# Layer 0's queries and keys written to DRAM ahead of the row maxima, layer 1's high and low parts a unit later, and the second router's norm derived from the first variance

## The reference, cut to what matters

```python
x = L0_attn_x
xn = _layernorm(x)
x = x + _L0_attn_ref(xn, ...) + _L0_ffn_ref(xn, ...)
xn = _layernorm(x)
x = x + _L1_attn_ref(xn, ...) + _L1_ffn_ref(xn, ...)
```

```python
mu = jnp.mean(x, axis=-1, keepdims=True)
var = jnp.var(x, axis=-1, keepdims=True)
xn = (x - mu) * jax.lax.rsqrt(var + LN_EPS) * ln_scale + ln_bias
logits = xn @ router_w.T + router_b
top_w, top_idx = jax.lax.top_k(logits, TOP_K)
```

## Time and profile before

| | |
|---|---|
| median of three runs | 497.09 us (496.85 to 499.26) |
| the profiled execution's own time | 498.41 us |
| its span in the profile | 496.7 us |
| granted TensorE clock, mean | 0.988 of full speed |
| busy: PE / weight loads / DVE / ACT / POOL | 88% / 62% / 65% / 48% / 37% |
| chain that ended last | PE 58%, DMA 12%, DVE 12%, issue 6%, SP's queue 4%, ACT 4% |

### The profile page before, as it was taken

How to read it: one execution, slowest core, us unless ns; L and a number is a source line. 1 busy time by engine, 2 the same in 40 slices (tenths; PEclk the granted TensorE clock), 3 DMA queues, 4 the chain that set the end, 5 groups by cost and what they waited for, 6 DMA issues and landing times.

```text
span 496.7 us, 9940 instructions
## 1 busy us (share of the span) xinstructions
PE 436.3 (88%) x3263; PEld 307.8 (62%) x3263; DVE 321.8 (65%) x988; ACT 240.1 (48%) x565; POOL 184.9 (37%) x234
## 2 busy tenths in 40 slices
PE   2568899997999899999999997999997999999985
PEld 1444446765666576665656655566557998998642
DVE  4554770117587777787877788767564666776665
ACT  2511355443655556553645435455463555555562
POOL 6570010002152543544445441666430444444100
PEclk9999999999999999999999999999997999999999
DMA  6447062323364653632236452142242122211233
GB/s 172 137 102 180 15 193 63 110 83 114 83 178 117 156 162 82 176 121 84 83 100 225 147 158 84 42 133 75 65 119 69 54 71 60 71 52 35 59 110 107
DMA packets 55216, 52.76 MB, mean 106 GB/s; under 512 B 5312, under 2 KB 50000, under 8 KB 55168
## 3 DMA queue, kind: packets, MB, share of 16 engines
q1 hardware_dynamic: 44208, 35.12, 25.4%
q10 hardware_dynamic: 8528, 12.03, 8.2%
q0 software_dynamic: 2432, 5.01, 3.4%
HBM read 33.09 MB, written 19.04 MB: 105 GB/s over the span
## 4 chain that ended last, share of the span: by engine, by line
PE 58%; DMA 12%; DVE 12%; issue 6%; SPq 4%; ACT 4%; POOL 3%; DVEq 0%; ACTq 0%; POOLq 0%
PE ps_P L1611 6%; PE ps_N L1743 5%; DMA scm<-MS 5%; DMA scr<-XQ 4%; PE ps_N L1544 4%; PE ps_M L1784 3%; PE ps_M L1753 3%; PE ps_P L1753 3%; PE ps_S L1743 3%; PE ps_M L1654 3%; PE ps_S L1589 3%; PE ps_N L1555 2%; PE ps_N L1550 2%; DVE NM L1140 2%; PE ps_S L1575 2%
## 5 line engine op out<-in xcount | busy, mean ns | idle before, releaser
L885 ACT ACTIVATE PT<-ps_S 128x512 f32<-128x512 f32 x192 | 112.3, 591 | 80.5 <-PE ps_S L1589 39.3
L1140 DVE TENSOR_REDUCE NM<-ps_N 128x2 f32<-128x512 f32 (+1 forms) x192 | 127.2, 680 | 35.5 <-PE ps_N L1550 22.7
L737 POOL TENSOR_SCALAR_AFFINE_SELECT PT<-PT 128x512 f32<-128x512 f32 x80 | 49.0, 636 | 139.2 <-ACT PT L885 139.2
L1544 PE MATMUL ps_N<-maskb,identb 128*128 128x256 bf16 (+1 forms) x192 | 62.0, 323 | 2.6 <-DVE NM L1140 1.7
L803 POOL DMA_INDIRECT yt<-LATE,EI x39 | 38.9, 997 | 56.3 <-DVE LATE L1378 46.6
L1611 PE MATMUL ps_P<-PT,VA 128*16 128x256 f32 (+1 forms) x1024 | 54.0, 328 | 0.4 <-ACT PT L885 0.4
L1550 PE MATMUL ps_N<-NS 96*128 96x512 f32 x96 | 52.8, 554 | 0.0
L1555 PE MATMUL ps_N<-NS 96*128 96x256 f32 (+1 forms) x128 | 49.4, 427 | 0.0
L1589 PE MATMUL ps_S<-NS 100*128 100x512 f32 (+1 forms) x96 | 46.2, 485 | 1.6 <-ACT PT L885 1.6
L1611 PEld LDWEIGHTS ps_P<-PT,VA 128*16 128x16 f32 x1024 | 23.3, 96 | 34.3 <-issue 20.5
L987 ACT ACTIVATE LATE<-ps_N,ucol 128x128 f32<-128x128 f32 x104 | 29.8, 369 | 27.4 <-PE ps_N L1743 26.0
(11 more groups left out here) (197 smaller groups left out, 845.1 us busy)
## 6 DMA issues: line engine op xcount, KB each, us to landing
scr<-XQ SPq DMA_DIRECT2D x24, 256.0 KB
NS<-scr SPq DMA_DIRECT2D x64, 96.0 KB
ROT<-in_L_ffn_W SPq DMA_DIRECT2D x16, 256.0 KB, 3.1
EW<-in_moe ACTq DMA_DIRECT2D x8, 512.0 KB, 3.8
scr<-XQ SPq DMA_DIRECT2D x24, 128.0 KB
NS<-scr SPq DMA_DIRECT2D x8, 384.0 KB
TS<-scr ACTq DMA_DIRECT2D x8, 384.0 KB
TS<-scr ACTq DMA_DIRECT2D x32, 96.0 KB
```

Of the source, the lines that this page charges most:

```text
L737: last = pool.affine_select(out=v, in_=v, compare_op=ALU.is_ge, fill=0.0, base=0, pattern=[[0, 4], [1, P]], channel_multiplier=-1)
L885: act.activation(PT[:, n % NPT, r, :], bank[s][:], ACT.Exp, scale=SCALE).then_inc(exp_ok, 1)
L1140: dve.tensor_reduce(to, x, AX.X, ALU.max, negate=True).then_inc(nm_ok, 1)
L1544: mm(diag, identb[:], maskb[:, None, :].broadcast_to((P, many, P)), start=True, stop=False, skip_group_check=True)
```

## The change

Three things change. First, the plan: in layer 0 `lo` comes behind unit 0's maximum and exponential and no longer ahead of them; in layer 1 `hi` moves from unit 0 to unit 1 (behind its exponential) and `lo` from the start of unit 1 to unit 2 (behind its maximum). Second, the item `stack` is split: `store` issues the four writes to scr, and `stack` waits for them and reads back. In layer 0 `store` stands ahead of `mrow` of half 1; in layer 1 it stands behind it, where the writes were. The reads of `again` move from units 3 to 7 to units 5 to 9. Third, the second norm: the variance of XN is now computed as v * rstd * rstd on two numbers per row, and its mean is taken as zero, so one fused instruction per tile makes the logits.

```diff
         for u in range(12):
             if u == 0:
                 add("qk", a)
-                add("hi", a)
-            if a and u == a[0]:
-                add("lo", a)
+                if t < NB:
+                    add("hi", a)
...
             add("max", b, u)
             add("exp", c, u // 3, u % 3)
+            if u == 0 and t < NB:
+                add("lo", a)
+            if u == 1 and t >= NB:
+                add("hi", a)
+            if u == 2 and t >= NB:
+                add("lo", a)
...
             if u == 1:
+                if t < NB:
+                    add("store", a)
                 add("mxt", c, 1)
                 add("mrow", c, 1)
+                if t >= NB:
+                    add("store", a)
                 add("stack", a)
                 add("ocp", d, 1)
...
-            if 3 <= u < 8 and b and b[0] == 0:
-                add("again", b, u - 3)
+            if 5 <= u < 10 and b and b[0] == 0:
+                add("again", b, u - 5)
...
-            def stack(L, b):
+            def store(L, b):
 
                 n = seq(L, b)
                 rows = P if L == 0 else NKV * HD
...
                 sp.dma_start(scr[L][b][1][0:rows, 2, :], xq[0:rows, 2, :]).then_inc(scr_w, 16)
+
+            def stack(L, b):
+
+                n = seq(L, b)
                 sp.wait_ge(scr_w, 64 * (n + 1))
...
-                pool.tensor_scalar(vpe[:, s], mv2[:, s, 1], EPS, 1.0, ALU.add, ALU.mult).then_inc(vpeb_ok, 1)
+                pool.tensor_scalar(vpe[:, s], var2[:, s], EPS, 1.0, ALU.add, ALU.mult).then_inc(vpeb_ok, 1)
...
-                dve.tensor_copy(rc[:, 0, :], bank["M0"][:, 0:E1])
-                dve.tensor_tensor(rc[:, 1, :], bank["M0"][:, E1:2 * E1], rbb[:], ALU.add).then_inc(rc_ok, 1)
+                dve.tensor_tensor(rc[:], bank["M0"][:, 0:E1], rbb[:], ALU.add).then_inc(rc_ok, 1)
...
-                dve.wait_ge(xnb_ok, 2 * b + 2)
-                for i in (2 * b, 2 * b + 1):
-                    last = dve.bn_stats(stats2[:, i, :], XN[:, i, :])
-                link(last)
-                for i in (2 * b, 2 * b + 1):
-                    last = dve.bn_aggr(mv2[:, i, :], stats2[:, i, :])
-                last.then_inc(mvc_ok, 1)
+
+                s = slice(2 * b, 2 * b + 2)
+                link(dve.tensor_tensor(var2[:, s], mv[:, s, 1], rstd[:, s], ALU.mult))
+                dve.tensor_tensor(var2[:, s], var2[:, s], rstd[:, s], ALU.mult).then_inc(mvc_ok, 1)
...
-                link(dve.tensor_tensor(dlt[:, s, :], bc(mv2[:, s, 0:1]), bc(rc[:, 0:1, :]), ALU.mult))
-                dve.tensor_tensor(ex[:, s, :], bank[f"M{b % 2}"][:, 0:2 * E1].rearrange("p (a e) -> p a e", e=E1), dlt[:, s, :],
-                                  ALU.subtract).then_inc(lg1_ok, 1)
+                for q in range(TPB):
+                    i = 2 * b + q
+                    last = dve.scalar_tensor_tensor(out=lg[:, i, :], in0=bank[f"M{b % 2}"][:, E1 * q:E1 * (q + 1)],
+                                                    scalar=rstd2[:, i:i + 1], in1=rc[:], op0=ALU.mult, op1=ALU.add)
+                last.then_inc(lg1_ok, 1)
                 dve.wait_ge(lg1_ok, b + 1)
-                link(dve.tensor_tensor(dlt[:, s, :], ex[:, s, :], bc(rstd2[:, s, None]), ALU.mult))
-                link(dve.tensor_tensor(lg[:, s, :], dlt[:, s, :], bc(rc[:, 1:2, :]), ALU.add))
...
-                mm(M0[:, 0:E1], ones, rwS[:], start=True, stop=True)
-                mm(M0[:, E1:2 * E1], ones, rwB[:], start=True, stop=True).then_inc(full["M0"], 1)
+                mm(M0[:, 0:E1], ones, rwB[:], start=True, stop=True).then_inc(full["M0"], 1)
```

More of the change, by code:

```diff
@@ L361, in build @@
         rbb = sb("rbb", [P, E1])
-        rc = sb("rc", [P, 2, E1])
+        rc = sb("rc", [P, E1])
         stats = sb("stats", [P, NT, 6])
@@ L368, in build @@
         mhalf = sb("mhalf", [P, NT])
-        stats2, mv2 = sb("stats2", [P, NT, 6]), sb("mv2", [P, NT, 2])
+        mv2, var2 = sb("mv2", [P, NT, 2]), sb("var2", [P, NT])
         rstd2 = sb("rstd2", [P, NT])
@@ L631, in attention @@
                 for item in plan:
+                    if item[0] == "store":
+                        store(*item[1:])
                     if item[0] == "stack":
@@ L1260, in normalise_x @@
                         .then_inc(xnb_ok, 1)
-                dve.wait_ge(xnb_ok, 2 * b + 2)
-                for i in (2 * b, 2 * b + 1):
-                    last = dve.bn_stats(stats2[:, i, :], XN[:, i, :])
-                link(last)
-                for i in (2 * b, 2 * b + 1):
-                    last = dve.bn_aggr(mv2[:, i, :], stats2[:, i, :])
-                last.then_inc(mvc_ok, 1)
+                s = slice(2 * b, 2 * b + 2)
+                link(dve.tensor_tensor(var2[:, s], mv[:, s, 1], rstd[:, s], ALU.mult))
+                dve.tensor_tensor(var2[:, s], var2[:, s], rstd[:, s], ALU.mult).then_inc(mvc_ok, 1)
             def logits(b):
-                s = slice(2 * b, 2 * b + 2)
-                def bc(x):
-                    return x.broadcast_to((P, TPB, E1))
                 await_full(dve, f"M{b % 2}", ("pl", 1, b))
                 dve.wait_ge(rstdc_ok, b + 1)
-                dve.wait_ge(mvc_ok, b + 1)
                 dve.wait_ge(rc_ok, 1)
-                link(dve.tensor_tensor(dlt[:, s, :], bc(mv2[:, s, 0:1]), bc(rc[:, 0:1, :]), ALU.mult))
-                dve.tensor_tensor(ex[:, s, :], bank[f"M{b % 2}"][:, 0:2 * E1].rearrange("p (a e) -> p a e", e=E1), dlt[:, s, :],
-                                  ALU.subtract).then_inc(lg1_ok, 1)
+                for q in range(TPB):
[3 more added lines that the diff above has]
+                last.then_inc(lg1_ok, 1)
                 dve.wait_ge(lg1_ok, b + 1)
-                link(dve.tensor_tensor(dlt[:, s, :], ex[:, s, :], bc(rstd2[:, s, None]), ALU.mult))
-                link(dve.tensor_tensor(lg[:, s, :], dlt[:, s, :], bc(rc[:, 1:2, :]), ALU.add))
                 for i in (2 * b, 2 * b + 1):
```

## The result

The changed kernel takes 494.65 us in the median of 17 runs (492.27 to 495.73), the kernel before 498.21 beside it; the ratio is 0.992, interval 0.9903 to 0.9937, so 0.6 to 1.0% faster. The time lies on the forecast of 494.6 us, but the forecast took 2.4 us off a median of 497.09, and measured side by side the kernel before takes 1.1 us more than that and the change takes off 3.6.

The account below looks back on a forecast made before the run. PE, busy 88% of the span, was taken as the bound, with DVE's chain to the division a second critical path. 1.27 + 0.4 + 0.5 + 0.35 + 0.2 - 0.35 = 2.4 us off 497.09 gave 494.6 us, range 490.5 to 498.0.

Parts of the forecast that it names:

- of the 0.8 us only 0.12 are kept: Stages 8 to 11: PE's unit-2 wait of 0.8 us becomes a wait of `ott` for the division, gaining 0.12 per stage.
- The term of 0.5 us: Layer 1, stages 8 to 11: 4 x 0.12 = 0.5 us gained in all.
- Stages 13 and 14: Layer 1, stages 13 to 15: the wait for an exponential is at most 0.6 us; no gain credited.
- Stage 12: `rank` waits for DVE's values (VA), which stand behind the low part: 0.35 us lost, halfway between 0.06 and 0.70.
- 1.3 us to spare, no cost: Layer 0, stage 5: half 1's maxima, behind four writes, are read back by 160.1; PE needs them at 161.4.
- The two waits of 1.27 us: Starts of stages 5 and 6: waits for the maxima of 0.41 and 0.86 us should go, 1.27 us gained.
- 1.67 us credited: Layer 0: 1.27 us from the maxima waits at stages 5 and 6, plus 0.4 from earlier scores in stages 4 and 7.
- Second norm and constants: DVE saves 4 to 7 us in stages 4 to 11, nothing on PE's path; smaller router constants gain 0.2 us.
- SP's chain at the experts: Start of layer-1 experts: PE's 3.29 us wait for a load shrinks as SP's chain runs ahead, 0.35 us gained.
- Full recovery: Rival, layer 1: `ott` not held by the division, all 5.4 us of waits won, about 489.4 us; chance 0.17.
- Nothing left: Rival: layer-0 stage-start waits pass to ACT's later reads into TS, layer 1's remainder is noise, 496.3 us; chance 0.23.
- Maxima late: Rival, stages 2 to 7: slow writes make half 1 0.8 us late each, 4.8 us lost, 499.5 us; chance 0.12.

Follow-up runs that it names:

- third chip: The changed kernel, unedited, run again on another chip as the measure for variants there: 495.07 us, ratio 0.991 to the kernel before.
- the control: The kernel before, run again with no edit: 506.79 us, ratio 1.0028.
- norm only: The kernel before with only the second norm's shortcut and the smaller router constants, order of high, low, writes and reads as before: 502.52 us, ratio 0.9939.
- layer 1 only: The kernel before with only layer 1's high parts a unit later and low parts behind the third unit's maximum: 499.62 us, ratio 0.9883.

## Why the prediction was right, and where not

- **Layer 1, stages 8 to 11: right up to `ott`, and too small by a factor of four.** Exponentials first, MS earlier, low part between MS and the division, division 0.06 us later (measured 0.04), `ott` 0.12 earlier (measured 0.16): each step is in the rows. What was wrong is the sentence that "of the 0.8 us only 0.12 are kept". The stage doesn't end with `ott`; `po` follows, and before its weights had a wait of their own of 0.30 us for ys. With 0.16 of `ott` and 0.30 of that wait gone, `po` starts 0.45 earlier, and the stage is 0.45 shorter. The term of 0.5 us measured 2.0, in six executions. The wait of `ott` for the division, forecast at 0.5 to 0.9 us in each of the four, is 0.44 in two of them.
- **Stages 13 and 14**, credited with nothing, took 18.59 and 18.60 against 18.52 and 18.76: right.
- **Stage 12**: predicted 0.35 lost, 21.89 - 21.56 = 0.33 measured, and 21.88 on the third chip. `rank` waits 1.20 where it waited 0.25. With the low part behind the division it is 0.55.
- **Layer 0: the step that failed** is "1.3 us to spare, no cost" for the maxima behind four writes. The writes landed 3.6 us after the first one's issue in stages 6 and 7, as taken, but after 4.3 and 4.0 in stages 4 and 5 (5.3 to 6.9 with the old order). Half 1's read, taken at 1.9 us, needed 141.67 - 138.86 = 2.8 in stage 4, beside ACT's large read. And half 0's write needs 4.5 to 5.8 us in the four stages, beside the other reads, instead of the 3.8 to 4.1 in the control. The rule that the prediction took from the Trainium skill ("DMA: Bandwidth & Descriptors", "Queues, rings and completion order"), that a small write completes after the earlier writes of its DMA engine, agrees: the maxima's write lands 138.86 - 136.51 = 2.35 us after its issue behind the four, and 156.70 - 155.24 = 1.46 in the control, ahead of them. The waits moved to unit 6, smaller. The two waits of 1.27 us were also one execution's: the control has 0.44 in all. Of 1.67 us credited, stages 4 to 7 show 0.2 (76.9 in the mean of four executions with the old order, 76.7 in five with the new one, scattered by 1.5 and 0.9, so 0.2 is not clear of the scatter), stage 2 another 0.3 to 0.5 that I had not looked at. By stages, the new order loses 0.5 in stage 4, gains 0.5 in stage 6 and 0.3 in stage 7.
- **Second norm and constants**: 0.19 of 0.2 us; DVE's busy time fell by 5.4 us, within the forecast 4 to 7, and norm only's stages 8 to 11 (84.36 against 84.43) show nothing of it.
- **SP's chain at the experts**: the wait fell from 3.29 to 2.77, but it is 3.15 and 3.07 in the changed kernel's other executions, and 0.49 in the control. The 0.35 is not shown.
- **The sum.** Stages: 2.0 + 0.5 + 0.2 + 0.2 - 0.3 = 2.6 us. That is close to the forecast of 2.4 because terms missed in opposite directions: layer 1 gave 1.5 more, layer 0 and the experts' wait about that much less. The median fell by 3.6 and the ratio says 4.0 (3.1 to 4.8), so 2.4 was too small. That 494.65 lies on 494.6 is luck: the prediction started from 497.09, 1.1 us below the median of the longer series. (By its own sum it should also have said 497.09 - 2.4 = 494.7.)
- **The rivals.** Full recovery: no. Of the 5.4 us of waits 3.2 stand in stages 8 to 11, and these gave 2.0; with the low part moved they gave 3.4, so there it was nearer than I had it. The 2.2 us in stages 12 to 15 gave nothing that stages 12 to 14 show. Nothing left: no. Maxima late: seen in small, and in full with the reads where they were, there mostly by the read back and not by the writes.

**What stays open.** The parts' ratios alone add to 2.1% and the whole gives 0.8 to 1.2%; norm only has 3 us and layer 1 only 4 us beyond what their stages explain, and no run shows why. One part of such differences is seen: in the changed kernel's profile the experts' block is 1.8 us shorter than before because it has one stretch of 3.4 us at 1.2 GHz where before has two, and its tail is 2.0 us longer, with 10 us at 1.2 GHz where before has 4. Whether a kernel with fewer waits has fewer such stretches in the mean, one profile each can't tell.

## What to carry to other kernels

When a wait is removed in a full engine's stream, follow the stream to the last dependent instruction of the stage, not to the next one: what counts was where `po` starts, not where `ott` starts. Where DMAs through DRAM carry a small urgent piece, list what every queue issues in the same 5 us, since moving one queue's order without the other's made four stages 2 to 8 us longer here. And compare stretches, several executions of each, before crediting a wait that one profile shows.

## What the runs showed of the hardware

- Waits of 0.4 to 0.9 us for a DMA come and go between executions of the same order (0.41 and 0.86 before, 0.44 in the control, none in norm only), while stages 8 to 11 together repeat to 0.1 us: 84.3 to 84.4 in four executions with layer 1's old order, 82.4 to 82.5 in six with the new one.
- On three chips every kernel had waits of 1 to 4 us, whose releaser the profile calls remote, about once per stage from stage 12 on, on DVE or ACT or both, with waits of PE of 0.3 to 2.4 us beside many of them: stages 12 to 14 took 63 to 68 us there, and 59 to 60 in the profiles without them (before, changed, and all three of another chip). They fall in the part where POOL issues its indirect DMAs; the cause wasn't found.
- PE's granted clock went to 1.2 GHz for 3.4 us at a time behind idle times. Behind the 2.95 us in stage 3 it did so in all fourteen profiles (for 6.8 us in one, whose stage was 1.5 us longer); behind the wait of 2.3 to 2.6 us in stage 12 in eight of them, as after 2.29 us in the control, and not after 2.28 us at the same place in the changed kernel's.
- The four writes to DRAM, with the maxima's behind them and ACT's reads later, landed 3.6 to 4.3 us after the first one's issue; beside ACT's reads, in the old order, 5.3 to 6.9.
